# Cross-attention: the values product every second step, two key banks, GpSimd started by VectorE's sums

## The reference

```
q, k, v = (x @ Wq.T + bq), (ctx @ Wk.T + bk), (ctx @ Wv.T + bv)     # 16 heads of 16
scores  = clip(q k / sqrt(16), -50, 50), masked by context row
probs   = softmax(scores)
delta   = layernorm((probs v) @ Wo.T + bo scaled) * gamma + beta
x       = x + delta
```

## Time and profile before

| | |
|---|---|
| median of 3 runs | 1688.69 us (1687.89 to 1691.54) |
| profiled execution, its own time | 1688.59 us |
| its span | 1686.4 us |
| TensorE busy in the span | 1538.2 us, 91% |
| VectorE | 1406.1 us, 83% |
| ScalarE | 1123.4 us, 67% |
| GpSimd | 743.4 us, 44% |

### The profile page before, as it was taken

One profiled execution on the slowest core, in us unless ns is written; L12 is line 12 of the kernel. 1 busy time (PEld: TensorE's weight loads), 2 busy tenths in 40 slices (PEclk: granted clock), 3 DMA queues, 4 the chain that ended last, 5 costly groups with the idle time before them and its releaser, 6 DMA issues. The chain is left out here.

```text
span 1686.4 us, 44072 instructions
## 1 busy us (share of the span) xinstructions
PE 1538.2 (91%) x18002; PEld 1294.3 (77%) x18002; DVE 1406.1 (83%) x2505; ACT 1123.4 (67%) x2187; POOL 743.4 (44%) x725
## 2 busy tenths in 40 slices
PE   4999999998639999999999999999999999999456
PEld 4878888886418888888888888888888888888224
DVE  3788888887467888989989889888899898898597
ACT  1666666665437777777777777777777777776475
POOL 0466656665163443453444434434444344343014
PEclk9999999999869999999999999999999999999677
DMA  8000000000221111111111111111111111110001
GB/s 223 1 1 2 1 1 2 1 1 1 82 92 39 50 51 50 51 40 49 51 51 50 42 47 51 51 51 43 46 51 50 51 50 39 51 51 2 1 12 33
DMA packets 43289, 67.91 MB, mean 40 GB/s; under 512 B 9365, under 2 KB 41810, under 8 KB 42962
## 3 DMA queue, kind: packets, MB, share of 16 engines
q1 hardware_dynamic: 43090, 65.11, 13.3%
HBM read 63.26 MB, written 1.84 MB: 39 GB/s over the span
## 5 line engine op out<-in xcount | busy, mean ns | idle before, releaser
L1115 POOL TENSOR_TENSOR xa_CW<-xa_CTX,xa_CH 128x500 fp32r<-128x500 f32 x187 | 307.1, 1642 | 591.2 <-ACT xa_CH L1309 591.2
L1337 DVE TENSOR_TENSOR xl_ACC<-xl_ACC,xl_PB 125x896 f32<-125x896 f32 x320 | 439.1, 1372 | 11.0
L1301 ACT ACTIVATE xl_PB<-banks,xl_BIB,xl_SCB 125x896 f32<-125x896 f32 x384 | 401.4, 1096 | 31.6 <-PE banks L1173 31.6
L1328 DVE TENSOR_SCALAR xl_PB<-xl_PB 125x896 f32<-125x896 f32 x384 | 249.0, 648 | 64.5 <-ACT xl_PB L1301 63.5
L1283 ACT ACTIVATE xl_V<-banks 125x256 f32<-125x256 f32 x384 | 147.9, 385 | 154.8 <-PE banks L1140 154.8
L1140 PE MATMUL banks<-xa_WVhigh,xa_CH 128*125 128x256 f32 x768 | 238.5, 311 | 0.0
L1140 PE MATMUL banks<-xa_WVlow,xa_CH 128*125 128x256 f32 x768 | 215.8, 281 | 0.0
L1140 PE MATMUL banks<-xa_WVhigh,xa_CW 128*125 128x256 f32 x768 | 215.7, 281 | 0.0
L1274 ACT ACTIVATE xl_KXhigh<-banks,xa_bk 128x500 fp32r<-128x500 f32 x192 | 130.5, 680 | 100.3 <-PE banks L1140 100.3
L1189 PE MATMUL banks<-xl_PB,xl_V 125*32 125x112 f32 x6144 | 187.2, 262 | 1.5 <-DVE xl_PB L1328 1.5
L1344 DVE SCALAR_TENSOR_TENSOR xl_KXlow<-banks,xa_bk,xl_KXhigh 128x500 fp32r<-128x500 f32 x192 | 137.5, 716 | 55.0 <-ACT xl_KXhigh L1274 54.2
(11 more groups left out here) (223 smaller groups left out, 3779.4 us busy)
## 6 DMA issues: line engine op xcount, KB each, us to landing
xa_CTX<-in_ctxT SPq DMA_DIRECT2D x93, 500.0 KB, 3.6
fw_QUT<-in_W_quT SPq DMA_DIRECT2D x1, 2048.0 KB, 13.2
fw_WO<-in_W_o SPq DMA_DIRECT2D x1, 2048.0 KB, 19.0
xq_WR<-in_w_gating SPq DMA_DIRECT2D x1, 2048.0 KB, 9.0
X<-in_x SPq DMA_DIRECT2D x1, 1792.0 KB, 9.7
out<-ff_R SPq DMA_DIRECT2D x16, 112.0 KB, 1.9
xa_CTX<-in_ctxT SPq DMA_DIRECT2D x1, 1500.0 KB, 14.4
xq_WL<-in_w_linear SPq DMA_DIRECT2D x1, 1024.0 KB, 11.3
```

What stands on the lines that cost most here:

```text
L1115: nc.gpsimd.tensor_tensor(context_piece(CW, i), context_piece(CTX, i), context_piece(CH, i), ALU.subtract).then_inc(ctx_low, 1)
L1301: nc.scalar.activation(PB[t % PR][:, :, :], banks[0:TK, 2 * i:2 * i + KT, 0:QW], ACT.Exp, scale=SCB[j][:, t:t + 1], bias=BIB[j][:, t:t + 1 ...
L1328: nc.vector.tensor_scalar(pt, pt, E_HI, E_LO, ALU.min, ALU.max).then_inc(clipped, 1)
L1337: nc.vector.tensor_tensor(ACC[j][:, :, :], prev[:, :, :], PB[t % PR][:, :, :], ALU.add).then_inc(summed, 1)
```

## The change

1. The values product runs every second step (u = 0, 2, 4 on TensorE) over the four tiles of the two steps before; `PR` is 6 and the values of a step share one bank and one copy.
2. The keys use two banks in turn, and wait for the low keys of the step before instead of the latest. The projection is behind the keys of step 3 (in one of these banks), and its read in step 4; the norm's steps move with it.
3. ScalarE reads the first heads of output and denominators in one operation (`first_heads`), VectorE the second heads in one.
4. GpSimd's operations wait for VectorE's sums: the low part for the second sum of the step, spreads and delta operations for the first. The queries are spread one part at u = 0 and one at u = 3. The mask columns are copied by ScalarE.
5. The norm's mean and variance are written in place without a copy.

```diff
-PR = 4
+PR = 6
-    V_BANK, O_BANK, K_BANK = (4, 5), 6, 7
+    V_BANK, O_BANK, K_BANK = 4, 6, (5, 7)
+    D_BANK = K_BANK[1]
-    PROJECT, NORM, ADD_DELTA = 3, {4: (0, 1), 5: (2,), 6: (3,), 10: (4, 5), 11: (6,)}, (6, 8, 9)
+    PROJECT, NORM, ADD_DELTA = 3, {5: (0, 1), 6: (2,), 7: (3,), 11: (4, 5)}, (7, 8, 10)
+    SPREAD = (0, 3)
...
# GpSimd, one step
+                        if u in SPREAD and not (last and j == 1):
+                            pool.wait_ge(summed, b * AC + 2 * u)
+                            spread_queries(ng, nj, b + 1, (SPREAD.index(u),))
+                        if s in ADD_DELTA and not first:
+                            if s not in (j * STEPS + w for w in SPREAD):
+                                pool.wait_ge(summed, b * AC + 2 * u)
+                            add_delta(g - 1, ADD_DELTA.index(s))
                         if more(last, s, C_AHEAD):
                             i = (s + C_AHEAD) % STEPS
                             pool.wait_ge(ctx_high, g * 2 * STEPS + s + 1)
+                            pool.wait_ge(summed, b * AC + 2 * u + 1)
                             nc.gpsimd.tensor_tensor(context_piece(CW, i), context_piece(CTX, i), context_piece(CH, i), ALU.subtract).then_inc(ctx_low, 1)
...
# TensorE
-                    pe.wait_ge(v_ready, n * 2 + 2)
-                    for i in range(2):
+                    pe.wait_ge(v_ready, n + 1)
+                    for i in range(-2, 2):
...
-                            if pu == 0 and not (first and j == 0):
-                                pe.wait_ge(d_read, b)
-                            values_product(n - 1, pu)
+                            if pu == 1 and not (first and j == 0):
+                                pe.wait_ge(o_read, b)
+                            if pu % 2 == 1:
+                                values_product(n - 1, pu)
                             if pu == STEPS - 1:
                                 denominators(b - 1, 1 - j)
                         if more(last, s, 1):
-                            values(n + 1, (u + 1) % STEPS, (0,))
-                        if s == PROJECT and not first:
-                            pe.wait_ge(k_ready, n + K_AHEAD)
-                            project(g - 1)
-                        if more(last, s, 1):
-                            values(n + 1, (u + 1) % STEPS, (1,))
+                            values(n + 1, (u + 1) % STEPS)
                         if more(last, s, K_AHEAD):
-                            pe.wait_ge(k_ready, n + K_AHEAD)
-                            if s == PROJECT and not first:
+                            pe.wait_ge(k_ready, n + K_AHEAD - 1)
+                            if s == PROJECT + 1 and not first:
                                 pe.wait_ge(delta_ready, g)
...
                             keys(n + K_AHEAD, i)
+                        if s == PROJECT and not first:
+                            pe.wait_ge(k_ready, n + K_AHEAD)
+                            project(g - 1)
...
-                    if p:
-                        pe.wait_ge(k_ready, p)
+                    if p >= 2:
+                        pe.wait_ge(k_ready, p - 1)
# ScalarE
+                def mask_columns(g, j, b):
+                    at = bass.ds(g * 2 * TILES + j * TILES, TILES)
+                    nc.scalar.activation(SCB[j][:, :], SCL[:, at], ACT.Copy)
+                    nc.scalar.activation(BIB[j][:, :], BIA[:, at], ACT.Copy).then_inc(mb_ready, 1)
+                def first_heads(b):
+                    act.wait_ge(pv_done, (b * STEPS + STEPS) // 2)
+                    act.wait_ge(den_done, b + 1)
+                    if b:
+                        act.wait_ge(o_read, b)
+                    nc.scalar.activation(OM[:, :, :], output_by_head()[:, :, 0, :], ACT.Copy, scale=D2[:, 0:1]).then_inc(o_half, 1)
...
+                            act.wait_ge(v_done, n + 1)
+                            nc.scalar.activation(V[:, t:t + 2, :], bank[V_BANK][0:TK, 0:2 * H].rearrange("t (i h) -> t i h", i=2), ACT.Copy).then_inc(v_ready, 1)
+                        if u == 0 and not (first and j == 0):
+                            first_heads(b - 1)
-                        if s == 5 and not first:
+                        if s == 6 and not first:
                             delta_rstd(g - 1)
+                        if u == 4 and not (last and j == 1):
+                            mask_columns(g + j, 1 - j, b + 1)
```

More of the change, by code:

```diff
@@ L1007, in cross_loop @@
         KX = [sb(f"KX{part}", [P, KT, CL], F32R) for part in ("high", "low")]
-        V = [sb(f"V{i}", [TK, H]) for i in range(PR)]
+        V = sb("V", [TK, PR, H])
         PB = [sb(f"PB{i}", [TK, KT, QW]) for i in range(PR)]
@@ L1089, in add_delta, with spread_queries @@
                         nc.gpsimd.tensor_tensor(xg, xg, DL[:, :].unsqueeze(1), ALU.add).then_inc(x_added, 1)
-                def spread_queries(g, j, b):
-                    for part in range(2):
+                def spread_queries(g, j, b, parts=(0, 1)):
+                    for part in parts:
                         q = QT[part][:, :, bass.ds(g * T + j * S, S)]
@@ L1148, in keys, with values @@
                     c, m = i // KT, i % KT
-                    split_products(bank[K_BANK][:, 0:CK], lambda a, kt: WK[a][:, kt, m * P:(m + 1) * P],
+                    split_products(bank[K_BANK[p % 2]][:, 0:CK], lambda a, kt: WK[a][:, kt, m * P:(m + 1) * P],
                                    lambda a, kt: ctx_parts[a][:, kt, c * CK:(c + 1) * CK]).then_inc(k_done, 1)
-                def values(n, u, tiles, early=False):
-                    for i in tiles:
+                def values(n, u):
+                    if n:
+                        pe.wait_ge(v_ready, n)
+                    for i in range(2):
                         t = 2 * u + i
-                        if not early:
-                            pe.wait_ge(v_ready, n * 2 + i - 1)
-                        split_products(bank[V_BANK[i]][0:TK, 0:H], lambda a, kt: ctx_parts[a][:, kt, t * TK:(t + 1) * TK],
-                                       lambda a, kt: WV[a][:, kt, :]).then_inc(v_done, 1)
+                        mm = split_products(bank[V_BANK][0:TK, i * H:(i + 1) * H], lambda a, kt: ctx_parts[a][:, kt, t * TK:(t + 1) * TK],
+                                            lambda a, kt: WV[a][:, kt, :])
+                    mm.then_inc(v_done, 1)
                 def scores(n, j, u, early):
@@ L1210, in project @@
                     for kt in range(KT):
-                        mm = nc.tensor.matmul(bank[K_BANK][0:T, 0:H], CN[:, kt, :], WO[:, kt, :], start=(kt == 0), stop=(kt == KT - 1))
+                        mm = nc.tensor.matmul(bank[D_BANK][0:T, 0:H], CN[:, kt, :], WO[:, kt, :], start=(kt == 0), stop=(kt == KT - 1))
                     mm.then_inc(delta_done, 1)
@@ L1273, in keys_high, with values_out @@
                     act.wait_ge(k_done, p + 1)
-                    nc.scalar.activation(KX[0][:, m, c * CK:(c + 1) * CK], bank[K_BANK][:, 0:CK], ACT.Identity,
+                    nc.scalar.activation(KX[0][:, m, c * CK:(c + 1) * CK], bank[K_BANK[p % 2]][:, 0:CK], ACT.Identity,
                                          bias=bk[:, m:m + 1]).then_inc(kh_ready, 1)
-                def values_out(n, u, early=False):
-                    if not early:
-                        act.wait_ge(pv_done, n - 1)
-                    for i in range(2):
-                        act.wait_ge(v_done, n * 2 + i + 1)
-                        nc.scalar.activation(V[(2 * u + i) % PR][:, :], bank[V_BANK[i]][0:TK, 0:H], ACT.Copy).then_inc(v_ready, 1)
+                def values_out(n, u):
+                    if n >= 3:
+                        act.wait_ge(pv_done, (n - 1) // 2)
+                    act.wait_ge(v_done, n + 1)
+                    t = 2 * u % PR
+                    nc.scalar.activation(V[:, t:t + 2, :], bank[V_BANK][0:TK, 0:2 * H].rearrange("t (i h) -> t i h", i=2), ACT.Copy).then_inc(v_ready, 1)
                 def pair(g, first, last):
@@ L1294, in pair @@
                             act.wait_ge(s_done, n * 2 + i + 1)
-                            if not (first and s < 2):
-                                act.wait_ge(pv_done, n - 1)
+                            if n >= PR // 2:
+                                act.wait_ge(pv_done, (n - 1) // 2)
                                 if t >= PR:
@@ L1317, in _ @@
                     if p == 1:
-                        values_out(0, 0, early=True)
+                        values_out(0, 0)
                 pairs(act, pair)
+                first_heads(B - 1)
                 delta_rstd(PAIRS - 1)
@@ L1418, in pair @@
                             await_step(g - 1, norm[0])
+                        if s == PROJECT + 1 and not first:
+                            read_delta(g - 1)
                         clip(n, 0, 2 * u)
                         add_tile(b, j, n, 0, 2 * u)
-                        if before and u == 0:
-                            read_output(b - 1)
```

(4 more changed lines are left out.)

76 lines of the change are left out of this document (23 added, 53 removed).

## The result

The changed kernel takes 1668.0 us (median of 4 runs, 1667.05 to 1669.2) where the kernel before took 1689.57 beside it on the same chip: a ratio of 0.9872 (0.9854 to 0.9891), so 21.6 us less, where 16.6 were forecast. As a time that is 1668.0 for the 1672.0 forecast; the stated range of the likeliest case was 1667 to 1677. Between the two profiled spans, 1686.4 and 1667.2 us, there are 19.2, and these 19.2 are what can be followed in the traces.

What follows compares the result with a forecast made beforehand. TensorE, busy for 899.03 of 900 us and waiting for nobody, was taken to bound the kernel. 10.3 + 5.4 + 1.3 + 0.3 - 0.7 = 16.6 us off 1688.6 gave 1672.0 us; range 1667 to 1677.

Steps and rivals of the forecast that it cites:

- the likeliest case: The forecast itself: 1667 to 1677 us, chance 0.60.
- The budget: Cross-attention loop: TensorE waits for nobody, so only its losses between its own instructions, or new waits, move the time.
- 1. Sections: Values product in the loop: 94 fewer sections, each saving 0.11 us on the way out, 10.3 us; bounds from 0.
- 2. Projection: Projection behind the keys: its wait and perhaps its restart go, 0.36 us x 15 = 5.4, bounds 3.5 and 7.4.
- 3. Start: Loop start: a second key bank removes a 1.54 us wait at the lower clock, saving 1.3 us, at best 1.5 plus.
- 4. Tail: Tail: fewer reads and one copy less, against norm statistics before the last clip; saves 0.3 us, bounds -0.5 and +1.
- 5. What costs nothing: ScalarE copies, heads, masks, values in one bank, buffers and context loads: no cost while TensorE covers them.
- 6. The wait that could take its place: Keys of odd steps reading GpSimd's low parts: worst place 0.5 us early; charged 0.7 us, bounds 0 and 1.5 per pair.
- Nearly all sums at 1.09: Sign expected in the profile after: VectorE's sums mostly undisturbed at 1.09 us, where the mean was 1.372.
- relief: Argument against late low parts: none begins before a sum any more, where some 0.29 of the sums were held.
- (b): Low parts partly late, keys of steps 9 and 11 wait 0.3 us each: 1681, range 1677 to 1685; chance 0.20.
- (d): Slower: waits past 1.35 us per pair, two further sums held at steps 7 and 8: 1693 us; chance 0.07.

Runs made afterwards that it cites:

- e1: Changed kernel with the values product run in every step again, ring of six buffers kept: 1682.83 us, ratio 0.9969.
- e4: Changed kernel with the projection between values and keys, and the second and third keys at the start waiting for low keys again: 1670.32 us, ratio 0.9889.
- e5: Changed kernel with one bank for all keys again and the projection in the bank left free: 1671.4 us, ratio 0.9901.
- e8: Changed kernel with an extra, unread GpSimd addition of 112x256 ahead of the low part of step 8: 1674.59 us, ratio 0.9915.
- e9: Changed kernel with the values product every third step over six tiles and a ring of 12 buffers: 1671.83 us, ratio 0.9901.
- e12: e11 with one spread at step 0, one at step 3, behind first sums, and masks copied by ScalarE: 1685.14 us, ratio 0.9987.
- e6: Changed kernel without the wait of GpSimd's low parts for the second sum; spreads and delta operations still tied: 1693.1 us, ratio 1.0018.
- e2: Kernel before with only the values product every second step and a ring of six buffers: 1701.26 us, ratio 1.0074.
- e3: Changed kernel without any of GpSimd's waits for VectorE's sums (low parts, spreads, additions of delta): 1696.62 us, ratio 1.005.
- e11: Kernel before with the values product every second step and GpSimd's low parts waiting for the second sum: 1702.25 us, ratio 1.0082.
- e10: Kernel before with only GpSimd's low parts made to wait for the step's second sum: 1687.28 us, ratio 0.9996.

## Why the prediction was right, and where its terms were off

**The budget (right).** TensorE had no waits, and what moved was its own losses; the changed kernel has no wait of a matmul in the loop.

**1. Sections (mechanism right, size too small: the largest error in us).** The step of 4.47 came as read from the first step of the loop. The merged section takes 1.67, not 1.69, and 1.56 where the denominators follow, not 1.58: besides the way out, 0.02 of a start is saved. A pair of batches went from 66.46 to 65.34; less the projection's 0.28 that leaves 0.84 for six sections, 0.14 each, and 94 of them are 13 us for the 10.3 foretold. e1 bears it out: 13.3 in the loop. By the rule of the Trainium skill, "TensorEngine Tiling (Array Packing)", Key Properties, taken for a whole change at 0.2, it would have been 18.8; the trace has 0.14, nearer to the value taken than to that.

**2. Projection (size too large).** 0.28 per pair for 0.36, so 4.2 us for 5.4, inside the bounds. The middle was taken because no row showed whether the restart would be paid again; it is, and e4 shows it is paid at either place.

**3. Start (the step that was most off for its size).** 2.8 us for 1.3, outside its own bounds. The term took the clock to rise at the same moment as before. It does not: with the wait, TensorE goes to its upper level (2.4 GHz; the values' instructions begin 0.12 apart instead of 0.21) at about 506.9, without it at about 504.6, though its first keys began 1.5 later. TensorE after, and then before:

```profile
504.80 0.28 PE L1136 MATMUL banks<-xa_WVhigh,xa_CH 128*125 128x256 f32 x1
504.92 0.28 PE L1136 MATMUL banks<-xa_WVlow,xa_CH 128*125 128x256 f32 x1
```

```profile
506.44 0.41 PE L1140 MATMUL banks<-xa_WVhigh,xa_CW 128*125 128x256 f32 x1
506.65 0.41 PE L1140 MATMUL banks<-xa_WVhigh,xa_CH 128*125 128x256 f32 x1
...
507.06 0.28 PE L1140 MATMUL banks<-xa_WVhigh,xa_CW 128*125 128x256 f32 x1
507.18 0.28 PE L1140 MATMUL banks<-xa_WVhigh,xa_CH 128*125 128x256 f32 x1
```

Windows from 505 to 510 us, after and then before:

```profile
505.00:510.00 5.00, 5.00 (x49) 4.38 (x48) 1.65 (x3) 3.27 (x5) 0.00 (x0) 1.00 0.01 3
```

```profile
505.00:510.00 5.00, 5.00 (x36) 4.36 (x36) 0.89 (x2) 2.13 (x4) 0.00 (x0) 0.80 0.01 3
```

The granted clock is 1.00 for 0.80. So 1.54 of wait came back, some 0.4 of restart with it, and the other 0.9 are keys and values that ran at the upper level and not at the lower (the values alone from 2.17 to 1.41). e4 and e5, which have the wait again, bear it out: in e4 the values' pace changes at 505.4, again far behind its first keys (496.63). Over all profiled kernels the way from first keys to first scores is 7.4 to 8.3 in the seven without the wait and 10.4 to 11.1 in the seven with it.

**4. Tail.** 0.3, as foretold.

**5. What costs nothing (right in the whole).** ScalarE's copy of 512 columns takes 0.60, foretold 0.59; no wait came of the heads, the masks or the values in one bank.

**6. The wait that could take its place (right by a narrow margin, and partly for a wrong reason).** The worst place is where it was put, steps 8 to 9, with 0.36 us in place of 0.5, and e8 bears it out: 0.69 later costs 0.53, the difference of 0.33 and 0.2 of the keys' restart. The timeline that led there came out nearly whole: from the scores of step 6 (995.23) the second sum of step 8 ends at 18.37 (18.2 foretold), the low part at 19.80 (19.7; its own terms give 19.6) and the keys begin at 20.16 (20.20). The next place, step 11, has 0.51 for the 0.4 foretold, and is the one that e9 and e12 run into. What was wrong is what stands around it. "Nearly all sums at 1.09" is false: the mean is 1.209, since the spreads and the operations of delta still begin behind a first sum, beside the clip, and hold the sum behind it (51 of the 235 sums from 700 to 1400 us, by 0.42 or 0.61), and the low part now holds the next clip:

```profile
1013.72 0.72 DVE L1360 SCALAR_TENSOR_TENSOR xl_KXlow<-banks,xa_bk,xl_KXhigh 128x500 fp32r<-128x500 f32 x1
1014.45 1.06 DVE L1344 TENSOR_SCALAR xl_PB<-xl_PB 125x896 f32<-125x896 f32 x1
...
1022.04 1.05 POOL L1093 TENSOR_TENSOR X<-X,xl_DL 112x256 f32<-112x256 f32 x1 [1.69 <-DVE xl_ACC L1353]
1022.53 1.51 DVE L1353 TENSOR_TENSOR xl_ACC<-xl_ACC,xl_PB 125x896 f32<-125x896 f32 x1
```

And the 0.7 charged for waits was not paid. The "relief" that spoke against rivals (b) and (d) is no relief in sum (101 us held before and after). What keeps (b) and (d) away is, as e6 shows beside the changed kernel, the place of the holds: behind the second sum, where VectorE often has the read of low keys next, which is not held (0.72 at 1013.72), and only then a clip. Where they fall in front of sums instead (e2, e3, e6), rival (d) comes true in size, 1693 to 1701. For the main edit alone it would have been the right forecast.

**The balance.** Foretold 10.3 + 5.4 + 1.3 + 0.3 - 0.7 = 16.6. Measured in the trace 13.3 + 4.2 + 2.8 + 0.3 - 0 = 20.6, less 1.5 by which the stages ahead of the loop happened to be later: 19.1, for 19.2 between the spans. That the time was met within 4 us is in part luck: the projection was put 1.2 too high, the sections 3.0 and the start 1.5 too low, and 0.7 was charged for waits that did not come. And it hung on the low part's tie, with 0.36 us to spare: without it (e6) rival (d) comes true.

**What is open.** In e12, how much of the last 0.97 per pair is the later NORM, and how much the projection's read, is read from waits and not shown apart. Whether the four reads of output and denominators on VectorE cost anything in this rhythm is open too.

## What to carry to other kernels

Where an engine is busy for all of the span, count how often it changes its shape of work: here every section of 32-column tiles less was worth 0.14 us, and nothing else about the work had to change. Merging makes the rhythm uneven, so look first at what the second engine does in the short step; here the gain of 13 us by itself was a loss of 12 until GpSimd's low parts began behind the second sum, and until the two spreads no longer ran back to back and held VectorE twice in a row (e11, e12). And a tie that is worth next to nothing by itself (e10) can be what the gain rests on: undo such parts one at a time in the changed kernel, not only add them one at a time to the old one.

## What the runs showed of the hardware that was not expected

**A clip waits for GpSimd's whole rest, as a sum does.** The end of the VectorE operation stands at a fixed distance behind the end of the GpSimd operation that ran when it began. From 700 to 1400 us of the changed kernel's timeline that holds for all 51 such sums, 0.94 to 0.96 behind (1024.04 behind 1023.09 in the rows of point 6), and for the clips, 0.47 to 0.52 behind (1015.51 behind 1015.03), but for nine. These nine began 0.03 or less behind GpSimd's own start (beside the addition of beta, at 1011.42, one at 1011.44); they took their 0.62, and it was GpSimd's operation that got longer, 1.24, where e8's addition of the same 112x256 takes 0.74. In the kernel before a clip is 0.49 behind in the earlier trace rows, 1080.73 and 1080.24. Alone, sum and clip take 1.09 and 0.62, so 0.14 of each runs beside the other engine and the rest behind it. The prediction had taken the 0.77 of the clip in the earlier trace rows for a mild slowing; it was the whole rest of the multiply. The rule of the Trainium skill, "GPSIMD Engine Reference", Key points, is that the two contend when VectorE reads two SBUF tensors or runs a two-port mode. The sums, which read two, agree with it; for the clips it needs a two-port mode, which no row names, though they take 0.62 for the 896 columns on which a sum spends 1.09.

**A second GpSimd operation right behind the first holds the sum too in one case and not in another.** In e6 a sum that began beside an operation of delta was held through it and the low part at its heels, and ended 0.96 behind the second (1038.25 and 1037.29). In e11, with the two spreads, the sum ended 0.95 behind the first (1027.23 and 1026.28) and the second spread got longer instead, 1.78 for 1.3. What decides between the two is not shown.

**VectorE's read of the low keys, which takes one operand from PSUM, is not held.** In the same stretch it takes 0.63 to 0.74 us beside a low part and 0.70 to 0.73 where none ran when it began, and 0.64 in the earlier trace rows. So behind the second sum a low part has about half of its 1.28 behind it before the next clip begins (1013.75 and 1014.45), and holds VectorE for the rest only.

**Without the gap in the first keys the clock rose sooner**, by the numbers of point 3: one wait of 1.54 us cost 2.8.
